# Second attention: the maximum of a head pair as two reductions of one PSUM bank, with scores and shifted scores issued head by head

## The chip, the core and the metric

The kernel runs on one core of a Trainium2 chip. The metric is device time in microseconds, the median of several executions. The engines that matter are TensorE (matmuls; PE in the rows, PEld its weight loads), VectorE (DVE), ScalarE (ACT) and GpSimd (POOL). They run side by side and meet by semaphores. PSUM, where matmuls write, has eight banks of 512 fp32 values in each of 128 partitions. TensorE's clock has two levels here, 1.2 and 2.4 GHz; the profile shows the granted one as a share of 2.4.

## What is computed

Eight sequences of 256 tokens with 128 features pass four stages, each a normalisation, a layer and a residual: an attention by hyperbolic distance, a mixture of experts, a second attention, and the mixture again. Only the second attention is touched:

```python
def _L0_attn_b_ref(x, qkv_w, qkv_b, proj_w, proj_b):
    B, N, D = x.shape
    H, hd = (NHEAD, HEAD_DIM)          # 16, 8
    qkv = x @ qkv_w.T + qkv_b
    ...
    q = q * cos + _rotate_half(q) * sin
    k = k * cos + _rotate_half(k) * sin
    attn = jnp.einsum('abhqd,abhkd->abhqk', q, k) * hd ** (-0.5)
    attn = jax.nn.softmax(attn, axis=-1)
    out = jnp.einsum('abhqk,bhkd->abhqd', attn, v)
    out = jnp.swapaxes(out, 1, 2).reshape(B, N, D)
    return out @ proj_w.T + proj_b
```

The softmax subtracts each query's maximum over its 256 keys. The kernel computes all scores twice for that: once with the queries on the partitions, to take the maximum along the free axis, and once with the keys on the partitions and the maximum already subtracted inside the matmul (`q2` holds the queries with an extra row of minus the maximum). The second form is what the exponential and the product with the values need.

## The kernel before

The order of work is written out by hand: each engine has its own program, and semaphores tie them. The second attention handles 8 samples (sequences) with 16 heads of 8 features. Heads go in pairs, `UNITS` = 8 pairs a sample, 64 in all. A head lies in a strip of 32 partitions, and a tile matmul uses 32 rows of TensorE's array: pair U uses row groups `j0` and `j0 + 1`, where `j0` is 0 for even pairs and 2 for odd ones.

TensorE (`samples_b`, line 728) first scores `AHEAD` = 13 pairs. Then in step U it issues the shifted scores of pair U and the scores of pair V = U + 13 (`b_tiles`, line 671), half of a value product for pair U - 3 or U - 4 (`pv_b`, line 719: eight matmuls), and, at three steps of every eight, a part of the maxima of a sample (`b_max_step`): a transpose, then two selections that spread the maxima over the rows of `q2`.

Scores go to banks 0 and 1, one for each head of the pair, with the two halves of the queries side by side (`b_score_step`, line 659). These banks are single: the next pair's scores wait until VectorE has read them (`s_mx`). Shifted scores go to banks 2 and 3 or 4 and 5, alternating (`b_shifted_step`, line 665), and wait for ScalarE's exponential of two pairs before (`s_e`). V and U have opposite parity, so that scores and shifted scores of one step lie on different row groups.

VectorE (`samples_b`, line 1501) reduces banks 0 and 1 in one instruction (`head_max`, line 1502) and, between the pairs, does the small work on the maxima: `max_split` after the eighth pair, `max_rows` after the next, and `shift` (an addition of 128x512 from PSUM) after the two that follow. ScalarE takes the exponential of the pair's 1024 columns (line 1009) and every fourth step copies a product out (line 1000). GpSimd and the DMA queues have no work that the stage waits for.

Of the kernel before, what the change touches and what calls it, by code (L numbers as in the profile page):

```python
# [7 lines left out]
ALU = mybir.AluOpType  # L8
ACT = mybir.ActivationFunctionType
AX_X = mybir.AxisListType.X  # L10
# [12 lines left out]
UNITS = H // 2  # L23
CHUNKS = H // 4
MT = N // P
# [36 lines left out]
def hybrid(nc, x, consts, wA, wB, bqk, brow, rwT, wexp, out):  # L62
    ctx = ExitStack()

    def sem(name):
        return ctx.enter_context(nc.semaphore(name))
# [3 lines left out]
    with ctx:  # L70
# [26 lines left out]
        def bank(n, k=1):  # L97
            return ps[:, 512 * n:512 * (n + k)]

        with ExitStack() as att:  # L100
# [40 lines left out]
            with ExitStack() as att_b:  # L141
                def sb_(name, shape, dt=F32):
                    return att_b.enter_context(nc.sbuf_tensor(name, shape, dt))
                q2 = [sb_(f"q2{k}", [P, CHUNKS, N], F32R) for k in range(2)]
                mx = sb_("mx", [P, CHUNKS, 4, MT])
# [135 lines left out]
        s_s1 = sem("b_scores_in_psum")  # L281
        s_mx = sem("b_max_read")
# [5 lines left out]
        s_s2 = sem("b_shifted_in_psum")  # L288
# [51 lines left out]
        def tok(s, m=0, n=N):  # L340

            return slice(s * N + m, s * N + m + n)
# [85 lines left out]
        def _(pe):  # L428
            def mm(o, l, r, start=True, stop=True, **kw):
                return pe.matmul(o, l, r, start=start, stop=stop, **kw)  # L430

            def rows(j):
                return slice(32 * j, 32 * (j + 1))
# [225 lines left out]
            def b_score_step(U, nt, i):  # L659

                s, c, j0 = U // UNITS, U % UNITS // 2, 2 * (U % 2)
                return mm(bank(i)[:, nt * N:(nt + 1) * N], qt[rows(j0 + i), c, tok(s, nt * P, P)],
                          kt[rows(j0 + i), c, tok(s)], tile_position=(32 * (j0 + i), 0))

            def b_shifted_step(U, mt, i):

                s, c, j0 = U // UNITS, U % UNITS // 2, 2 * (U % 2)
                return mm(bank(2 + 2 * (U % 2) + i)[:, mt * N:(mt + 1) * N], kt[rows(j0 + i), c, tok(s, mt * P, P)],
                          q2[s % 2][rows(j0 + i), c, :], tile_position=(32 * (j0 + i), 0))

            def b_tiles(U, V):

                shifted, scores = 0 <= U < B * UNITS, V < B * UNITS
                if shifted and U % UNITS == 0:
                    pe.wait_ge(s_q2, 2 * (U // UNITS) + 2)
                if shifted and U >= 2:
                    pe.wait_ge(s_e, U - 1)
                if scores and V >= 1:
                    pe.wait_ge(s_mx, V)
                for half in range(MT):  # L680
                    if shifted:
                        b_shifted_step(U, half, 0)
                        last = b_shifted_step(U, half, 1)
                        if half == MT - 1:
                            last.then_inc(s_s2, 1)
                    if scores:
                        b_score_step(V, half, 0)
                        last = b_score_step(V, half, 1)
                        if half == MT - 1:
                            last.then_inc(s_s1, 1)  # L690

            def b_max_transposed(s):

# [34 lines left out]
            def samples_b():  # L728
                for V in range(AHEAD):
                    b_tiles(-1, V)  # L730
                    b_max_step(V)
                for U in range(B * UNITS + 3):
                    V = U + AHEAD
                    b_tiles(U, V)
                    if U >= 3:
                        pv_b((U - 3) // 2, (U - 3) % 2)
                    if V < (B + 1) * UNITS:
                        b_max_step(V)
# [519 lines left out]
        def _(dve):  # L1258
# [242 lines left out]
            def samples_b():  # L1501
                def head_max(U):
                    c, j0 = U % UNITS // 2, 2 * (U % 2)
                    dve.wait_ge(s_s1, U + 1)
                    dve.tensor_reduce(mx[:, c, j0:j0 + 2, :], bank(0, 2).rearrange("p (i t m) -> p i t m", i=2, t=MT),  # L1505
                                      AX_X, ALU.max).then_inc(s_mx, 1)

                def max_split(s):

                    dve.wait_ge(s_mx, UNITS * (s + 1))  # L1510
                    if s >= 1:
                        dve.wait_ge(s_mT, s)
                    rows = mtok[:, :, :].rearrange("p t (j x) -> p t j x", x=32)[:, :, :, 0:8]
                    rows = rows.rearrange("p t j (c e) -> p t j c e", e=2)
                    whole = mx[:, :, :, :].rearrange("p c j t -> p t j c")
                    st.do(dve.tensor_scalar(rows[:, :, :, :, 0], whole, -1.0, None, ALU.mult))
                    st.sync()
                    for t in range(MT):
                        last = dve.scalar_tensor_tensor(rows[:, t, :, :, 1], whole[:, t], -1.0, rows[:, t, :, :, 0],
                                                        ALU.mult, ALU.subtract)  # L1520
                    last.then_inc(s_ms, 1)

                def max_rows(s):
                    dve.wait_ge(s_mT, s + 1)
                    if s >= 1:
                        dve.wait_ge(s_mq, 2 * s)
                    dve.tensor_copy(mxT[:, :], bank(7)[:, 0:N]).then_inc(s_mr, 1)

                def shift(s, half):
                    dve.wait_ge(s_mq, 2 * s + half + 1)  # L1530
                    if s >= 2:
                        dve.wait_ge(s_s2, UNITS * (s - 1))
                    cs = slice(2 * half, 2 * half + 2)
                    dve.tensor_tensor(q2[s % 2][:, cs, :], bank(7).rearrange("p (c n) -> p c n", c=2),  # L1534
                                      qt[:, cs, tok(s)], ALU.add).then_inc(s_q2, 1)

                dve.wait_ge(s_sel, 3)
                for V in range((B + 1) * UNITS):
                    if UNITS <= V < B * UNITS and V % UNITS == 0:
                        dve.wait_ge(s_ms, V // UNITS)  # L1540
                    if V < B * UNITS:
                        head_max(V)
                    s, at = V // UNITS - 1, V % UNITS
                    if at == UNITS - 1 and V < B * UNITS:
                        max_split(s + 1)
                    elif at == 0 and s >= 0:
                        max_rows(s)
                    elif at in (1, 2) and s >= 0:
                        shift(s, at - 1)
# [265 lines left out]
```

## Time and profile before

| | us |
|---|---|
| median of 3 runs | 1306.38 (1305.45 to 1308.87) |
| the profiled execution | 1306.9 |
| its span, first to last instruction | 1305.1 |
| TensorE busy / VectorE busy / ScalarE busy over the span | 1015.4 / 1020.3 / 735.0 |
| VectorE's maxima of the second attention (line 1505) | 64 x 1224 ns, 78.3 busy |
| VectorE idle ahead of them, most of it until TensorE is done | 40.7 |
| ScalarE's exponentials (line 1009) | 64 x 1023 ns, 65.4 busy, 58.7 idle ahead of them |

The profile is one execution. The second attention's scores begin near 779 us and its last value product ends near 944. The busy shares over the whole span say little about it, since the two mixtures of experts fill most of the time with dense matmuls; it has to be read in its own stretch. Idle time is put down to the instruction that ended it. Durations of matmuls overlap: the distance between starts tells the pace, and a matmul's own row holds its way through the array too.

### The profile page before, as it was taken

Reading aid. Unit: us, or ns where it says so; the run is one execution under the profiler, and the core shown is the slowest. Engines: PE = TensorE matmul, PEld = TensorE weight load, DVE = VectorE, ACT = ScalarE, POOL = GpSimd, SP = SyncE. Lnnn points to the kernel's source line nnn. Section 1 sums busy time; section 2 is a strip of 40 time slices with the busy share of each in tenths; the row PEclk is TensorE's granted clock in tenths of the full one; section 3 lists DMA queues with packets and bytes.
Section 4 is the critical chain, followed back from the end, with each engine's and each line's share of the span. In section 5 each row is a group of like instructions: output and inputs, shape, how many; then the busy total and the mean of one; then the engine's idle time right before and its main releaser. Section 6 shows DMA issues by size and latency. Waiting matters only on the chain. (4 is left out here: it accounts for less than half of the span.)

```text
span 1305.1 us, 17528 instructions
## 1 busy us (share of the span) xinstructions
PE 1015.4 (78%) x5292; PEld 706.6 (54%) x5292; DVE 1020.3 (78%) x1720; ACT 735.0 (56%) x886; POOL 324.0 (25%) x217
## 2 busy tenths in 40 slices
PE   4655666666643799999999664778962899999997
PEld 3433333334322577787777332333451777877776
DVE  4347988888827799999998766666157799999997
ACT  2323999999952355555555221555521555555554
POOL 2002655555530122222222320000000122222221
PEclk8665555555555799999999775776575899999999
DMA  1000000000000366666664000000000566666664
GB/s 48 1 1 0 1 1 1 1 1 1 1 7 8 91 153 153 148 150 149 145 149 94 29 1 0 1 2 1 1 7 8 130 152 146 148 149 140 146 149 103
DMA packets 26090, 85.24 MB, mean 65 GB/s; under 512 B 3904, under 2 KB 17088, under 8 KB 17856
## 3 DMA queue, kind: packets, MB, share of 16 engines
q1 hardware_dynamic: 26048, 84.70, 28.4%
q8 instruction: 25, 0.41, 0.1%
q14 instruction: 17, 0.14, 0.0%
HBM read 82.58 MB, written 2.10 MB: 65 GB/s over the span
## 5 line engine op out<-in xcount | busy, mean ns | idle before, releaser
L1061 ACT ACTIVATE sg<-ps 128x512 f32<-128x512 f32 x264 | 157.8, 599 | 127.3 <-PE ps L430 127.3
L1067 ACT ACTIVATE hh<-hf 128x512 fp32r<-128x512 f32 x264 | 167.0, 633 | 104.6 <-DVE hf L1691 104.3
L430 PE MATMUL ps<-xh,whi 128*128 128x512 f32 x528 | 207.6, 393 | 0.0
L430 PE MATMUL ps<-xh,wlo 128*128 128x512 f32 x528 | 207.4, 393 | 0.0
L430 PE MATMUL ps<-xl,whi 128*128 128x512 f32 x528 | 207.0, 392 | 0.0
L1685 DVE TENSOR_TENSOR hl<-hf,hh 128x512 fp32r<-128x512 f32 x264 | 186.3, 706 | 26.3 <-ACT hh L1067 6.7
L1165 POOL TENSOR_TENSOR rr<-xr,rr 128x2048 f32<-128x2048 f32 x32 | 144.9, 4545 | 211.9 <-ACT xr L952 207.7
L1691 DVE TENSOR_TENSOR hf<-h,cbc 128x512 f32<-128x512 f32 x256 | 195.0, 762 | 0.0
L1678 DVE TENSOR_TENSOR h<-sg,ps 128x512 f32<-128x512 f32 x264 | 179.4, 680 | 18.3 <-PE ps L430 8.1
L1209 POOL CAST whi<-wraw 128x384 fp32r<-128x384 f32 x66 | 61.7, 935 | 480.3 <-PE ps L430 377.6
L430 PE MATMUL ps<-hh,whi 128*128 128x512 f32 x264 | 110.7, 419 | 7.8 <-DVE hl L1685 7.8
L430 PEld LDWEIGHTS ps<-xh,whi 128*128 128x128 f32 x528 | 100.0, 189 | 23.0 <-DVE h L1678 0.5
L430 PEld LDWEIGHTS ps<-xl,whi 128*128 128x128 f32 x528 | 100.0, 189 | 22.2
L430 PEld LDWEIGHTS ps<-xh,wlo 128*128 128x128 f32 x528 | 99.7, 189 | 21.7
L1505 DVE TENSOR_REDUCE mx<-ps 128x4 f32<-128x1024 f32 x64 | 78.3, 1224 | 40.7 <-PE ps L430 39.9
L430 PE MATMUL ps<-hl,whi 128*128 128x512 f32 x264 | 103.8, 393 | 0.0
L430 PE MATMUL ps<-hh,wlo 128*128 128x512 f32 x264 | 103.8, 393 | 0.0
L1009 ACT ACTIVATE wr<-ps 128x1024 f32<-128x1024 f32 x64 | 65.4, 1023 | 58.7 <-PE ps L430 58.3
L1211 POOL TENSOR_TENSOR wlo<-wraw,whi 128x384 fp32r<-128x384 f32 x66 | 87.7, 1329 | 5.3
L430 PE MATMUL ps<-qt,kt 32*128 32x256 f32 x256 | 50.8, 494 | 45.6 <-DVE xr L1368 44.9
L1368 DVE TENSOR_SCALAR xr<-ps 128x1024 f32<-128x1024 f32 x64 | 77.8, 1215 | 8.6 <-PE ps L430 8.6
L1376 DVE SCALAR_TENSOR_TENSOR xr<-ps,xr 128x1024 f32<-128x1024 f32 x64 | 78.2, 1221 | 4.3
(246 smaller groups left out, 1590.5 us busy)
## 6 DMA issues: line engine op xcount, KB each, us to landing
cbc<-routing_coefficients SPq DMA_DIRECT2D x128, 512.0 KB, 6.1
wraw<-in_wexp_dram SPq DMA_DIRECT2D x66, 192.0 KB, 5.9
X<-in_x_dram SPq DMA_DIRECT2D x4, 256.0 KB, 4.5
routing_coefficients<-cT SPq DMA_DIRECT2D x8, 128.0 KB, 2.3
out_dram<-X SPq DMA_DIRECT2D x4, 256.0 KB, 2.8
cstb<-in_consts_dram SPq DMA_DIRECT2D x1, 648.0 KB, 3.5
wa<-in_wA_dram SPq DMA_DIRECT2D x1, 256.0 KB, 3.9
wb<-in_wB_dram SPq DMA_DIRECT2D x1, 192.0 KB, 3.6
```

The lines of the kernel that those rows point to most:

```text
L430: return pe.matmul(o, l, r, start=start, stop=stop, **kw)
L1009: act.activation(wr[:, C % CHUNKS, U % 2 * UC:(U % 2 + 1) * UC], bank(2 + 2 * (U % 2), 2), ACT.Exp, scale=SCALE_B).then_inc(s_e, 1)
L1061: act.activation(sg[c % 2][:, :], bank(4 + 2 * (c % 2)), ACT.Silu).then_inc(s_sg, 1)
L1067: act.activation(hh[c][:, :], hf[c % 2][:, :], ACT.Copy).then_inc(s_hh, 1)
L1165: pool.tensor_tensor(rr[:, C % RR, :], xr[:, C % XR, :], rr[:, C % RR, :], ALU.add).then_inc(s_S, 1)
L1211: pool.tensor_tensor(wlo[slot][:, :], wraw[slot][:, :], whi[slot][:, :], ALU.subtract).then_inc(s_ws, 1)
L1368: dve.tensor_scalar(xr[:, C % XR, at], bank(0, 2), 0.0, None, ALU.max).then_inc(s_N, 1)
L1376: dve.scalar_tensor_tensor(xr[:, C % XR, at], bank(2, 2), R_MAX, xr[:, C % XR, at], ALU.min, ALU.mult).then_inc(s_X, 1)
L1505: dve.tensor_reduce(mx[:, c, j0:j0 + 2, :], bank(0, 2).rearrange("p (i t m) -> p i t m", i=2, t=MT), AX_X, ALU.max).then_inc(s_mx, 1)
L1678: dve.tensor_tensor(h1[c % 2][:, :], sg[c % 2][:, :], bank(5 + 2 * (c % 2)), ALU.mult).then_inc(s_h1, 1)
L1685: dve.tensor_tensor(hl[c][:, :], hf[c % 2][:, :], hh[c][:, :], ALU.subtract).then_inc(s_hl, 1)
L1691: dve.tensor_tensor(hf[c % 2][:, :], h1[c % 2][:, :], coefs, ALU.mult).then_inc(s_h, 1)
```

## The change

`head_max` takes the maximum by two reductions of one bank each, and raises `s_mx` after each, so that it counts heads. `s_s1` is raised after each head's scores. TensorE issues score and shifted score of head 0 for both halves, then, after another wait for `s_mx`, those of head 1. In the old order both heads' tiles of a half stood together, behind one wait. The counts of the waits follow: `max_split` waits for twice as many. No buffer, no other loop and no DMA changes.

```diff
@@ -675,19 +675,18 @@
                     pe.wait_ge(s_q2, 2 * (U // UNITS) + 2)
                 if shifted and U >= 2:
                     pe.wait_ge(s_e, U - 1)
-                if scores and V >= 1:
-                    pe.wait_ge(s_mx, V)
-                for half in range(MT):
-                    if shifted:
-                        b_shifted_step(U, half, 0)
-                        last = b_shifted_step(U, half, 1)
-                        if half == MT - 1:
-                            last.then_inc(s_s2, 1)
-                    if scores:
-                        b_score_step(V, half, 0)
-                        last = b_score_step(V, half, 1)
-                        if half == MT - 1:
-                            last.then_inc(s_s1, 1)
+                for i in range(2):
+                    if scores and V >= 1:
+                        pe.wait_ge(s_mx, 2 * (V - 1) + i + 1)
+                    for half in range(MT):
+                        if scores:
+                            last = b_score_step(V, half, i)
+                            if half == MT - 1:
+                                last.then_inc(s_s1, 1)
+                        if shifted:
+                            last = b_shifted_step(U, half, i)
+                            if half == MT - 1 and i == 1:
+                                last.then_inc(s_s2, 1)
 
             def b_max_transposed(s):
 
@@ -1501,13 +1500,14 @@
             def samples_b():
                 def head_max(U):
                     c, j0 = U % UNITS // 2, 2 * (U % 2)
-                    dve.wait_ge(s_s1, U + 1)
-                    dve.tensor_reduce(mx[:, c, j0:j0 + 2, :], bank(0, 2).rearrange("p (i t m) -> p i t m", i=2, t=MT),
-                                      AX_X, ALU.max).then_inc(s_mx, 1)
+                    for i in range(2):
+                        dve.wait_ge(s_s1, 2 * U + i + 1)
+                        dve.tensor_reduce(mx[:, c, j0 + i, :], bank(i).rearrange("p (t m) -> p t m", t=MT),
+                                          AX_X, ALU.max).then_inc(s_mx, 1)
 
                 def max_split(s):
 
-                    dve.wait_ge(s_mx, UNITS * (s + 1))
+                    dve.wait_ge(s_mx, 2 * UNITS * (s + 1))
                     if s >= 1:
                         dve.wait_ge(s_mT, s)
```

## Rows read from the trace of the kernel before

**Rows 1.** Chain of work that ended last, 778 to 950 us, shares by line.

```profile
by line: PE ps L430 51.5%; DVE mx L1505 35.8%; issue 4.4%; PE ps L698 2.5%; PE ps L748 2.3%; DVE q L1534 1.8%; ACT o_all L1000 0.4%; DVE b_otok L1561 0.3%; DVE b_rden L1557 0.2%; DVEq L1504 0.0%; DVEq L1554 0.0%
```

**Rows 2.** Timeline, pairs ahead: start, duration, engine, line, operation, count, idle and its releaser.

```profile
783.69 0.80 PE L430 MATMUL ps<-kt,qt 32*128 32x256 f32 x4 [1.32 <-DVE mx L1505]
784.53 1.23 DVE L1505 TENSOR_REDUCE mx<-ps 128x4 f32<-128x1024 f32 x1 [0.89 <-PE ps L430]
785.81 0.80 PE L430 MATMUL ps<-kt,qt 32*128 32x256 f32 x4 [1.32 <-DVE mx L1505]
```

**Rows 3.** First tiles of the first and of the 52nd step (chain, timeline).

```profile
807.12 0.85 PE ps L430 x8
...
916.74 0.79 PE L430 MATMUL ps<-q,kt 32*128 32x256 f32 x4
```

**Rows 4.** Timeline, a plain step at a granted clock of 0.50.

```profile
826.29 0.58 PE L430 MATMUL ps<-q,kt 32*128 32x256 f32 x2 [0.43 <-DVE mx L1505]
...
827.02 1.08 PE L430 MATMUL ps<-wr,vt 128*32 128x256 f32 x8
827.12 1.02 ACT L1009 ACTIVATE wr<-ps 128x1024 f32<-128x1024 f32 x1 [1.22 <-PE ps L430]
827.17 1.23 DVE L1505 TENSOR_REDUCE mx<-ps 128x4 f32<-128x1024 f32 x1 [1.02 <-PE ps L430]
...
828.54 0.58 PE L430 MATMUL ps<-q,kt 32*128 32x256 f32 x2 [0.43 <-DVE mx L1505]
```

**Rows 5.** Timeline of TensorE at a granted clock of 1.00, a selection and plain steps.

```profile
818.39 0.39 PE L430 MATMUL ps<-q,kt 32*128 32x256 f32 x2
...
818.83 0.64 PE L430 MATMUL ps<-wr,vt 128*32 128x256 f32 x8
819.40 0.50 PE L430 MATMUL ps<-mxT,mxs 128*128 128x256 f32 x2
820.34 0.39 PE L430 MATMUL ps<-q,kt 32*128 32x256 f32 x2 [0.44 <-DVE mx L1505]
...
822.30 0.39 PE L430 MATMUL ps<-q,kt 32*128 32x256 f32 x2 [0.88 <-DVE mx L1505]
```

**Rows 6.** Timeline of TensorE at 0.50: selections of two neighbouring steps.

```profile
902.82 0.80 PE L430 MATMUL ps<-mxT,mxs 128*128 128x256 f32 x2
...
905.28 0.80 PE L430 MATMUL ps<-mxT,mxs 128*128 128x256 f32 x2
```

**Rows 7.** Timeline of TensorE in the tail: products of two steps, and the closing run.

```profile
928.52 1.08 PE L430 MATMUL ps<-wr,vt 128*32 128x256 f32 x8
...
930.25 1.08 PE L430 MATMUL ps<-wr,vt 128*32 128x256 f32 x8
...
940.97 3.40 PE L430 MATMUL ps<-wr,vt 128*32 128x256 f32 x32
```

**Rows 8.** Timeline of VectorE: an addition of 128x512, the reduction behind it, a small operation.

```profile
818.35 0.69 DVE L1534 TENSOR_TENSOR q<-ps,qt 128x512 fp32r<-128x512 f32 x1
...
818.97 1.23 DVE L1505 TENSOR_REDUCE mx<-ps 128x4 f32<-128x1024 f32 x1
...
830.67 0.19 DVE L1516 TENSOR_SCALAR mtok<-mx 128x32 fp32r<-128x32 f32 x1
```

**Rows 9.** Timeline of TensorE in the preparation: two steps, each for four row groups.

```profile
755.92 0.51 PE L430 MATMUL ps<-b_qh,sel 32*128 32x512 f32 x4
756.26 0.41 PE L430 MATMUL ps<-b_ql,sel 32*128 32x512 f32 x4
```

**Rows 10.** Busy us by stretch: PE, PEld, DVE, ACT, POOL, then granted clock, DMA, GB/s.

```profile
813.70:817.70 4.00, 3.93 (x34) 1.73 (x34) 2.75 (x6) 1.75 (x2) 0.00 (x0) 0.50 0.00 0
817.70:824.50 6.80, 4.54 (x64) 2.35 (x60) 5.43 (x6) 3.86 (x5) 0.00 (x0) 1.00 0.01 2
...
899.60:903.00 3.40, 3.40 (x27) 1.22 (x24) 2.69 (x3) 1.99 (x2) 0.00 (x0) 0.50 0.01 2
...
952.00:960.00 8.00, 7.23 (x56) 6.38 (x56) 4.35 (x10) 0.60 (x2) 0.00 (x0) 1.00 0.00 0
```

## Prediction

> **What bounds the kernel now.** First I read the chain that ended last, over the stretch of the second attention (778 to 950 us). TensorE's one matmul line holds 51.5% of it and the maximum on VectorE 35.8% [rows 1]: the stage is a ping-pong of these two, and ScalarE's exponentials are almost nowhere on the chain. The timeline shows three parts.
>
> Thirteen head pairs are scored ahead, until 807.1 us. A pair is four matmuls, which take 0.83 us until the reduction starts; the reduction takes 1.23, and 0.05 later TensorE begins the next four [rows 2]. Nothing overlaps: 2.12 us a pair.
>
> Then 51 steps (807.1 to 916.7 us, 109.6 us or 2.15 a step [rows 3]), each with scores of pair V, shifted scores of pair U = V - 13 and eight value products. With TensorE granted 1.2 GHz, a plain step is 2.25 us: tiles from 826.29, products from 827.02 (0.73 for eight tile matmuls), reduction at 827.17, next tiles at 828.54, which is 0.14 after the reduction's end [rows 4]. At 2.4 GHz it is 1.96 (tiles at 820.34 and 822.30): products come after 0.44 and take 0.57 to the selection behind them [rows 5], and the reduction starts 0.58 after the tiles [rows 5, 8]. Three steps in eight also carry a transpose or a selection of the maxima. At 1.2 GHz those take 2.46, and TensorE is then busy throughout [rows 6].
>
> Last, 916.7 to about 944.4 us, the steps have no scores. TensorE sets their pace at 1.2 GHz: 1.73 us each, then a run of 3.4 us of products [rows 7].
>
> **The change part by part.** *The reduction.* One instruction of 1024 elements becomes two of 512. The nearest row of that size from PSUM is the addition of 128x512, 0.69 us, and the reduction behind it started 0.62 after it did [rows 8]. Half of 1.23, 0.61, is the lower bound, 0.69 the upper. I take 0.69 for the end that TensorE sees and 0.62 for the pitch of two in a row; the same element count makes the addition a close stand-in. VectorE then needs at least 1.24 us for a pair.
>
> *Scores ahead.* Head 0 of the next pair can be computed while head 1 is reduced. A head's own loop is 0.05 + 0.83 + 0.69 = 1.57 us, above VectorE's 1.24, so a pair takes about 1.6 where it took 2.12. That holds for ten of the thirteen. The others also carry VectorE's work on the maxima, two additions of 0.69 among it, which used to lie in VectorE's idle time; I count nothing for them. 10 x 0.5 = **-5 us**.
>
> *The order of the tiles.* The old order puts tiles of four row groups side by side. The new one issues score and shifted tile of head 0, the second half of both on the same two row groups, then head 1. If TensorE kept program order, the second halves would hold up head 1, and a step would have three rounds in place of two. One row speaks on this. In the preparation the program issues columns 0 and 1 of the query highs, then 0 and 1 of the lows, and only then columns 2 and 3. The trace has all four highs at 755.92 and all four lows at 756.26 [rows 9]: work for free row groups went past work for busy ones, past a wait already met as well. So eight tiles stay two rounds, 0.73 or 0.44 us, if head 1's wait is met; if not, head 1's rounds start when it is.
> The Trainium skill says otherwise (TensorE: Matmul & The Clock Gate, Part 3, "The mechanism"): only weight loads are pulled ahead, and matmuls start and end strictly in program order. By that rule the third round would be paid, which is the third rival below; the row disagrees with it.
>
> *Plain step at 1.2 GHz.* TensorE's own work is 0.73 + 1.02 = 1.75 us (the tail's pace, 1.73 [rows 7]). Let a step start with both heads' waits met: scores are there after 0.84, head 0 is reduced by 1.53, head 1 by 2.15 to 2.2. The next step starts at 1.75, its head 1 only at about 2.2, so it ends 1.75 later, near 3.95, a length of 2.2; the one after that meets no wait. Lengths alternate 1.75 and 2.2, mean 1.97, against 2.25.
> *Steps with transpose or selection at 1.2 GHz:* TensorE is full, 2.46 stays. Eight steps: 5 x 1.97 + 3 x 2.46 = 17.2 us, against 5 x 2.25 + 3 x 2.46 = 18.6 before and 8 x 2.15 = 17.2 as the trace has it with its share of fast clock. The lower clock alone gains nothing here.
>
> *Plain step at 2.4 GHz.* Scores after 0.54 to 0.58, TensorE's own work 0.44 + 0.57 = 1.01, VectorE 1.24. The same recurrence gives lengths of 1.36 and 1.52, mean 1.44, against 1.96. The three special steps add VectorE's two additions (1.24) and some small operations (0.19 the first [rows 8]), some 1.3 of which finds no slack (an estimate: the plain steps leave VectorE 0.2 each): eight steps 8 x 1.44 + 1.3 = 12.8 us.
>
> *The clock.* It rose to 2.4 GHz at 817.7, and at a like place in four more samples, right after TensorE had been busy 3.93 of 4.00 us at the transpose; a stretch just as full (3.40 of 3.40) brought no rise [rows 10]. It fell again after 6.8 us in which TensorE was busy 4.54, that is in plain steps of 1.96 [rows 5, 10]. The change keeps the full stretches and packs the same matmuls into steps of 1.44: 4.54/6.80 x 1.96/1.44 = 0.91. The stretch from 952 to 960 held 2.4 GHz with 7.23 of 8.00, 0.90 [rows 10]. So I expect a rise at the first to third sample and then mostly no fall.
> Main part, with 4 of its 6.4 samples at 2.4 GHz: 4 x 12.8 + 2.4 x 17.2 = 92.5, against 109.6: **-17 us**.
>
> *The tail.* The new order changes nothing by itself (two row groups, two rounds). At 2.4 GHz TensorE needs 1.01 a step, and ScalarE, with 1.02 for each exponential [rows 4] and every fourth step a copy of 128x512 (no dearer than the 0.69 of rows 8), about 1.2: 13 x 0.5 + about 1.7 of the closing products = **-8 us**. If the clock is low, nothing.
>
> *The added wait.* A third wait stands inside each step, with shifted tiles, products and selections queued behind it on TensorE. One wait costs 0.05 after its release [rows 2], two 0.14 [rows 4]. Met early it costs nothing; at 0.05 on each of some 60 steps **+3 us**, bound 0 to 0.14 each, 9 us. ScalarE's exponential waits for head 1's tiles: at most 0.5 late, and its 1.02 leaves over 0.9 idle in each plain step before [rows 4].
>
> Sum: -5 - 17 - 8 + 3 = -27 us. The profiled execution took 1306.9 us, 1305.1 of it the span; the median of the runs shown is 1306.4, so the forecast is 1306.4 - 27 = **1279 us**.
>
> **The rivals.** *1. The clock falls again in every sample.* For it: the old kernel did just that, 6.8 us high of the 17.2 of eight steps, two fifths. Eight steps take 1/(0.4/12.8 + 0.6/17.2) = 15.1 us, the main part 96.7: -13, -5 ahead, 0 in the tail, +3: **1292 us**. Against it: the denser steps.
> *2. It never rises.* -5 + 0 + 0 to 3: **1303 us**. For it: the stretch at 899.6, full and without a rise; against it five rises in seven samples.
> *3. Program order holds on TensorE.* A third round costs half of the two rounds' 0.73, 0.36 us at 1.2 GHz. A plain step is 1.75 + 0.36 = 2.11, a special one 2.82: eight steps 19.0, main part 6.4 x 19.0 = 121 (+12), tail 13 x 0.36 = +5, ahead -5, and I leave the clock low: **1318 us**. It decides against the change as soon as a second pair of row groups can't start beside the first. For it: the skill's rule; against it rows 9.
>
> **How the numbers follow.** Forecast 60%, rival 1 17%, rival 2 10%, rival 3 10%, the rest 3% for a wait inside the step that costs the whole gain. The low end is the high clock from the first sample with a free wait: 6.4 x 12.8 = 82 in the main part, 1306.4 - 28 - 5 - 8 = 1265. The high end takes in rivals 1 and 2: 1304. A measurement tells 0.3% (4 us) from no change: rivals 1 and the forecast are faster, rival 2 lies on the border, rival 3 is slower. Faster 81%, same 8%, slower 11%.
>
> **What would show it.** Right: reductions of 0.6 to 0.69 at twice the count; about 1.6 a pair ahead; eight tiles still 0.73 or 0.44 before the products; steps alternating; granted clock high through most of the stage and its tail; all else unmoved. Wrong: tiles in three rounds (1.1 at 1.2 GHz), reductions well over 0.69, or a clock that still falls in each sample.

## The result, and the profile after

The changed kernel takes 1267.1 us in the median of four executions (1263.9 to 1286.9), the kernel before beside it 1305.9: a ratio of 0.970, 95% interval 0.966 to 0.973. The forecast of 1279 had the sign and lies 12 us too high; the range of 1265 to 1304 holds the result. This ratio and those below leave out executions more than 1.5% above the fastest of the same kernel, here the one of 1286.9; the medians keep them.

I compare the two profiled executions (1306.9 and 1268.4 us; spans 1305.1 and 1266.5) by the points at which TensorE starts a new part, as in [rows 2, 3, 7]:

| part, us | before | after | forecast | measured |
|---|---|---|---|---|
| all before the first scores | 779.4 | 777.2 | 0 | -2.2 |
| 13 pairs ahead | 27.8 | 21.6 | -5 | -6.2 |
| 51 steps | 109.6 | 89.6 | -17 | -20.0 |
| tail | 28.3 | 19.5 | -8 | -8.8 |
| the added wait | | | +3 | inside the 51 steps |
| all behind | 360.0 | 358.6 | 0 | -1.4 |
| span | 1305.1 | 1266.5 | -27 | -38.6 |

So 35 of the 38.6 us come from the stage. The start of the first scores lies between 775 and 784 us in all the profiles here, changed or not, so the -2.2 in front of it is no effect of the change.

The page of the changed kernel gives the reductions and, by slices of 31.7 us, the granted clock. The stage fills the slices 25 to 29:

```profile
PEclk8665555555555599999999986589965999999999
L1505 DVE TENSOR_REDUCE mx<-ps 128x2 f32<-128x512 f32 x128 | 82.4, 686 | 11.6 <-PE ps L430 10.6
```

128 reductions of 0.686 us stand where 64 of 1.23 stood [rows 2]. The chain that ended last, over 778 to 911 us:

```profile
by line: PE ps L430 56.6%; DVE mx L1505 19.0%; issue 8.1%; DVE q L1534 4.1%; ACT wr L1008 2.6%; ACT o_all L999 2.3%; PE ps L747 1.7%; PE ps L697 1.7%; DVE mxT L1527 1.1%; ACT L1008 1.0%; DVE mtok L1519 0.7%; DVE mtok L1516 0.6%; DVE b_otok
```

The reduction held 35.8% of that chain [rows 1] and holds 19.0% now. The ping-pong shows as gone in the timeline of the pairs ahead (start, duration, engine, line, operation, count, idle and its releaser):

```profile
783.56 1.39 PE L430 MATMUL ps<-kt,qt 32*128 32x256 f32 x4 [0.18 <-DVE mx L1505]
784.38 1.29 DVE L1505 TENSOR_REDUCE mx<-ps 128x2 f32<-128x512 f32 x2 [0.28 <-PE ps L430]
785.13 1.39 PE L430 MATMUL ps<-kt,qt 32*128 32x256 f32 x4 [0.18 <-DVE mx L1505]
```

A pair is 1.57 us (783.56 to 785.13) where it was 2.12. TensorE idles 0.18 a pair instead of 1.32, VectorE 0.28 instead of 0.89 [rows 2]. Both reductions together take 1.29, hardly more than the old one's 1.23.

Next, TensorE in two plain steps at a granted clock of 0.50 (1.2 GHz), with the reductions between:

```profile
815.94 0.58 PE L430 MATMUL ps<-kt,qt 32*128 32x256 f32 x1
...
815.96 0.57 PE L430 MATMUL ps<-q,kt 32*128 32x256 f32 x1
...
816.32 0.41 PE L430 MATMUL ps<-kt,qt 32*128 32x256 f32 x1
...
816.68 1.08 PE L430 MATMUL ps<-wr,vt 128*32 128x256 f32 x8
816.77 1.29 DVE L1505 TENSOR_REDUCE mx<-ps 128x2 f32<-128x512 f32 x2 [0.87 <-PE ps L430]
...
817.69 0.58 PE L430 MATMUL ps<-kt,qt 32*128 32x256 f32 x1
...
818.07 0.41 PE L430 MATMUL ps<-kt,qt 32*128 32x256 f32 x1
...
818.12 0.58 PE L430 MATMUL ps<-kt,qt 32*128 32x256 f32 x1
...
818.84 1.08 PE L430 MATMUL ps<-wr,vt 128*32 128x256 f32 x8
...
819.85 0.58 PE L430 MATMUL ps<-kt,qt 32*128 32x256 f32 x1
```

The first step starts with both heads' waits met: first halves at 815.94 to 815.96, second halves at 816.32, products at 816.68, 0.74 after the first tile. Its length is 1.75. The second starts head 0 at 817.69, but head 1 only at 818.12, just after VectorE has left that bank, and lasts 2.16. These are the alternating 1.75 and 2.2 of the prediction; the old step was 2.25 [rows 4].

The same at 1.00 (2.4 GHz):

```profile
858.35 0.38 PE L430 MATMUL ps<-kt,qt 32*128 32x256 f32 x1
...
858.70 0.38 PE L430 MATMUL ps<-kt,qt 32*128 32x256 f32 x1
...
858.89 2.63 DVE L1505 TENSOR_REDUCE mx<-ps 128x2 f32<-128x512 f32 x4 [0.25 <-PE ps L430]
...
859.73 0.35 PE L430 MATMUL ps<-kt,qt 32*128 32x256 f32 x1
...
860.23 0.38 PE L430 MATMUL ps<-kt,qt 32*128 32x256 f32 x1
...
861.23 0.38 PE L430 MATMUL ps<-kt,qt 32*128 32x256 f32 x1
```

The steps start at 858.35, 859.73 and 861.23: 1.38 and 1.50, forecast 1.36 and 1.52, before 1.96 [rows 5]. VectorE runs four reductions in 2.63 and then idles 0.25 (from 861.52 to 861.77) until TensorE has the next tiles: it is busy for nine tenths of two steps and sets most of their pace, where TensorE and VectorE took turns before.

The clock, as busy time by stretch (columns as in [rows 10]):

```profile
777.00:799.00 22.00, 18.99 (x60) 13.66 (x62) 18.52 (x33) 0.00 (x0) 4.50 (x1) 0.50 0.00 0
799.00:831.30 32.30, 30.35 (x232) 15.40 (x232) 23.95 (x43) 17.62 (x19) 0.00 (x0) 0.50 0.00 1
831.30:888.00 56.70, 54.95 (x596) 29.81 (x598) 53.21 (x96) 40.24 (x45) 0.00 (x0) 1.00 0.01 2
888.00:907.80 19.80, 16.30 (x194) 7.67 (x186) 3.11 (x8) 16.31 (x19) 0.00 (x0) 1.00 0.00 1
```

It rose once, at 831.0, as the 16th of the 51 steps began (in the third sample whose scores fall into them), and stayed at 2.4 GHz through the steps and the tail. Before, it rose in five samples and fell in each.

### The profile page after: what moved, and what is told of

It is laid out like the page before. It is cut to its first block and busy times, and to the rows that moved or that the text cites. A ratio compares the mean times of both kernels' runs of the same rounds, so it can differ in the third digit from the quotient of the medians.

```text
span 1266.5 us, 17592 instructions
## 1 busy us (share of the span) xinstructions
PE 1006.7 (79%) x5292; PEld 714.6 (56%) x5292; DVE 1023.3 (81%) x1784; ACT 734.1 (58%) x886; POOL 324.2 (26%) x217
## 5 line engine op out<-in xcount | busy, mean ns | idle before, releaser
L1505 DVE TENSOR_REDUCE mx<-ps 128x2 f32<-128x512 f32 x128 | 82.4, 686 | 11.6 <-PE ps L430 10.6
L1008 ACT ACTIVATE wr<-ps 128x1024 f32<-128x1024 f32 x64 | 65.3, 1024 | 32.2 <-PE ps L430 32.0
```

The costliest lines, as they stand in the source:

```text
L1008: act.activation(wr[:, C % CHUNKS, U % 2 * UC:(U % 2 + 1) * UC], bank(2 + 2 * (U % 2), 2), ACT.Exp, scale=SCALE_B).then_inc(s_e, 1)
L1505: dve.tensor_reduce(mx[:, c, j0 + i, :], bank(i).rearrange("p (t m) -> p t m", t=MT), AX_X, ALU.max).then_inc(s_mx, 1)
```

## The experiments

Two theories stood at first. Mine: the reductions and the order of the tiles together let the engines overlap, and the denser TensorE keeps the clock, which then pays most. The rivals: the order alone costs (a third round of tiles), or the split alone gains, or the clock is the whole gain. Where a kernel carries extra matmuls, their results go to banks that are rewritten before anybody reads them.

**The order alone, with the old reduction** (against the kernel before).

```diff
                 if scores and V >= 1:
                     pe.wait_ge(s_mx, V)
-                for half in range(MT):
-                    ...
+                for i in range(2):
+                    for half in range(MT):
+                        if scores:
+                            last = b_score_step(V, half, i)
+                            ...
+                        if shifted:
+                            last = b_shifted_step(U, half, i)
```

> The kernel before with the new order of the tiles alone: one reduction of 1024 elements, one wait for it ahead of the step, then score and shifted tile of head 0 for both halves, then head 1. Theory (free row groups pass busy ones): eight tiles stay two rounds, 0.73 us at 1.2 GHz before the products, a plain step stays 2.25 or 1.96, time within 0.3% of before. Rival (program order holds): a third round of 0.36 us in each of 64 steps at 1.2 GHz, some 20 us slower.

Measured: 1307.5 us (median of 10, 1301.5 to 1312.2) beside 1307.5 for the kernel before, ratio 0.999 (0.996 to 1.001). TensorE at the start of one step, at 0.50:

```profile
833.70 0.58 PE L430 MATMUL ps<-kt,qt 32*128 32x256 f32 x1
833.71 0.58 PE L430 MATMUL ps<-q,kt 32*128 32x256 f32 x1
833.72 0.58 PE L430 MATMUL ps<-kt,qt 32*128 32x256 f32 x1
833.72 0.57 PE L430 MATMUL ps<-q,kt 32*128 32x256 f32 x1
834.08 0.41 PE L430 MATMUL ps<-kt,qt 32*128 32x256 f32 x1
...
834.10 0.41 PE L430 MATMUL ps<-kt,qt 32*128 32x256 f32 x1
```

The program issues head 0's first halves, head 0's second halves, then head 1's. The four first halves of both heads start within 0.02 us, the second halves 0.38 later. The rows don't name the head, but one pair of row groups runs one round at a time: in the changed kernel, where head 1 had to wait, head 0's second halves at 818.07 follow its first ones at 817.69 by 0.38. So four tiles at once are both heads', and head 1's first halves went past head 0's second ones, whose row groups were taken. Two rounds stay two, and the third rival (1318) is out. So is, for row-tiled matmuls, the sentence of the Trainium skill that the prediction set against it (TensorE: Matmul & The Clock Gate, Part 3, "The mechanism"): in strict program order head 1's tiles would have waited.

**The split alone, with the old order and one wait for both heads** (against the changed kernel).

```diff
-                for i in range(2):
-                    if scores and V >= 1:
-                        pe.wait_ge(s_mx, 2 * (V - 1) + i + 1)
-                    ...
+                if scores and V >= 1:
+                    pe.wait_ge(s_mx, 2 * V)
+                for half in range(MT):
+                    ...
```

> Two reductions of one bank with the old order of the tiles, and TensorE waits for both ahead of the step. Theory (the gain is the overlap of a head's scores with the other head's reduction): no gain, VectorE needs 1.29 us for a pair in place of 1.23, so 0.06 x 64 = 4 us slower. Rival (smaller reductions alone free the banks sooner): faster.

Measured: 1316.4 us (10; 1310.1 to 1323.1), ratio 1.007 (1.004 to 1.010): 9 us slower, where 4 were expected. A plain step at 0.50:

```profile
851.99 0.58 PE L430 MATMUL ps<-q,kt 32*128 32x256 f32 x2 [0.49 <-DVE mx L1506]
...
852.85 1.29 DVE L1506 TENSOR_REDUCE mx<-ps 128x2 f32<-128x512 f32 x2 [1.01 <-PE ps L430]
...
854.28 0.58 PE L430 MATMUL ps<-q,kt 32*128 32x256 f32 x2 [0.49 <-DVE mx L1506]
```

2.29 a step against 2.25: the 0.06 by which two reductions outlast one, some 4 us in 64 pairs. In this profile, the slowest of the ten executions, the clock also never rose in the stage, which took 176.0 us against 165.7; so the missing bursts of high clock can account for the rest, which one profile doesn't prove. Neither the order nor the split gains anything alone. With the wait per bank added to both, TensorE refills bank 0 while bank 1 is read. The wait was not taken apart from the order: a wait per bank in the old order, where head 0's second half is issued behind head 1's first, was not run.

**Extra full-width matmuls among the pairs ahead,** to have the clock up before the steps begin; on the changed kernel (shown) and, twice after each pair, on the one before.

```diff
+                    if U < 0:
+                        fill(2 * V + i)
+            def fill(n):
+                mm(bank(2 + n % 4), kt[:, 0, 0:P], qt[:, 0, 0:2 * N])
```

> The changed kernel with two matmuls of 128x128 by 512 columns added to each pair that is scored ahead, into banks that nobody reads and that the shifted scores overwrite later. They serve no result. Theory (the clock is the larger part of the gain, and the denser steps keep it): it rises to 2.4 GHz during the 13 pairs ahead and stays, the pairs take about 1.35 us, all 51 steps about 1.6 on average; 1255 to 1259 us, some 10 below the changed kernel. Rival (the clock depends on chance or falls again for another reason): within 3 us of the changed kernel, or slower by what the added matmuls take, 13 x 2 x 0.2 to 0.4 us.

> The kernel before with the same added matmuls in the pairs ahead. Theory (plain steps of 1.96 us do not keep the clock): it is high in the pairs ahead, 3 to 4 us gained there, and falls in the steps as before; 1301 to 1305 us. Rival (a clock once high stays high whatever the steps are): main part 51 x 2.0 = 102 and tail 19, 1285 us or less.

Measured: 1286.6 (4; 1282.5 to 1292.1) and 1305.9 (10; 1303.9 to 1311.1), beside 1307.5. The aim was missed. TensorE of the first of them:

```profile
790.57 0.79 PE L430 MATMUL ps<-kt,qt 32*128 32x256 f32 x2
791.29 0.80 PE L430 MATMUL ps<-qt,kt 128*128 128x512 f32 x1
```

Row tiles and full-width matmuls follow each other at 0.72, a pair takes 2.9 us instead of 1.57, and the clock stayed at 0.50 until 829 us although TensorE was busy 39.00 of the 39.00 us from 781 to 820. The part ahead grew to 38.9 us; but with the clock up from 829 on, the 51 steps took 83.6 and the tail 19.5. On the kernel before, four of the five bursts of high clock came as they had (from 834.3, 851.4, 868.4 and 885.5 us), the first, at 817.7, did not, and the stage took 168.0. That run tells nothing on a clock that is once high, since it never was in the part ahead.

**The changed kernel again,** in two further sets of executions, to see how steady it is.

> The changed kernel, unchanged, for more executions beside the next three. Theory (the gain hangs on when the granted clock rises, which differs between executions): its times spread more than the 0.3% of before, from about 1264 to 1290 us, median near 1267. Rival (one disturbed execution among four): all within 0.3% of 1267.

> The changed kernel once more beside the two, on the same chip: 1263 to 1287, median near 1270.

Measured: 1273.6 (6; 1263.4 to 1286.3), ratio 0.974 (0.970 to 0.978), and 1278.3 (4; 1268.1 to 1294.7), ratio 0.973 (0.968 to 0.979). The first set was a favourable draw. Over all 14 executions it lies between 1263.4 and 1294.7, median 1269.6, where all executions of the kernel before lie between 1301 and 1319, with medians of 1306 to 1309. The granted clock over the whole span mostly goes with it: 0.797 at 1268.1, 0.774 at 1286.5, 0.760 at 1294.7, though 0.786 at 1286.9. The slowest is a profile in which the clock never rose in the stage; its steps and its tail by stretch:

```profile
797.50:907.00 109.50, 107.53 (x830) 52.23 (x832) 79.58 (x139) 59.28 (x64) 0.00 (x0) 0.50 0.00 1
907.00:935.00 28.00, 27.42 (x186) 11.78 (x186) 2.47 (x7) 15.87 (x19) 0.00 (x0) 0.50 0.00 1
```

Here the 51 steps take 109.3 us, the tail 28.6, the part ahead 21.6: the gain in the steps and the tail is gone and the -6 ahead is left. This is the second rival, which the prediction gave one chance in ten, at 1303 us; of the 12 us by which this execution is faster than the profiled one before, 6 lie outside the stage. With the clock low throughout, the steps of the split alone took 119.1, and eight steps of the order alone at 0.50 took 18.46 (824.65 to 843.11) where eight take 17.3 here, 7 us over 51 steps. So the overlap is worth 7 to 10 us in the steps even at 1.2 GHz; the kernel before had its 109.6 with a mean granted clock of 0.66.

**The kernel before with its clock kept up** by extra value products that change nothing: 8 to 16 after each pair ahead and 8 in each plain step.

```diff
+            def fill(n, where):
+                for k in range(n):
+                    j = k % 4
+                    mm(bank(where)[rows(j), ...], vt[:, 0, 0:VW],
+                       kt[:, 0, 0:N].bitcast(F32), tile_position=(0, 32 * j))
...
                     b_tiles(-1, V)
+                    fill(16 if V < 3 else 8, 6)
...
+                    if V < B * UNITS and V % UNITS >= 3:
+                        pe.wait_ge(s_q2, 2 * (V // UNITS))
+                        fill(8, 7)
```

> The kernel before, with the same added matmuls in the pairs ahead and 8 more in each of the five plain steps of a sample, into the bank of the maxima while that is free. They serve no result. Theory (clock and overlap are two gains, and the clock alone is worth less): granted clock high throughout, plain steps 1.96, main part 101 us in place of 110, tail 19 in place of 28; 1285 to 1290 us, so 20 to 25 slower than the changed kernel. Rival (the clock is all of the gain): 1270 or less. If the clock does not stay high, a plain step costs 2.8 and the kernel is some 20 us slower than before.

Measured: 1285.0 us (4; 1283.6 to 1288.4) beside 1306.3, ratio 0.984 (0.982 to 0.986). Its steps, and a step at a granted clock of 1.00:

```profile
803.00:903.00 100.00, 89.48 (x1356) 46.09 (x1356) 74.47 (x89) 59.07 (x64) 0.00 (x0) 1.00 0.01 2
```

```profile
852.13 0.39 PE L430 MATMUL ps<-q,kt 32*128 32x256 f32 x2
...
852.71 1.22 DVE L1515 TENSOR_REDUCE mx<-ps 128x4 f32<-128x1024 f32 x1 [0.73 <-PE ps L430]
...
853.03 1.04 PE L430 MATMUL ps<-kt,vt 128*32 128x256 f32 x16
854.08 0.39 PE L430 MATMUL ps<-q,kt 32*128 32x256 f32 x2
```

The old step stays at 1.95, as in [rows 5], and the 16 products lie in TensorE's idle time. The clock alone is worth 21 us: 99.8 in the steps, 18.6 in the tail. The changed kernel in the same set took 1273.6, 11 us less, with plain steps of 1.44 and pairs of 1.57 for 1.95 and 2.12. That the clock is the whole gain is refuted.

Four profiles of these experiments, set side by side, part the two gains. The stage, from its first scores to the part behind it, took, in us:

| | clock never high | clock high in the steps and the tail |
|---|---|---|
| no overlap | 176.0 (split alone) | 146.3 (before, kept up) |
| overlap | 159.5 (changed, slowest) | 127.2 (changed, clock up from the second step, last experiment) |

The overlap is worth 16.5 us at the low clock (some 4 of them the split's own price) and 19.1 at the high one, the clock 29.7 and 32.3. Both gains stand by themselves, and the clock is the larger. The kernel before (165.7) already had part of it from its bursts.

**The same extra products in the part ahead of the changed kernel only.**

```diff
                     b_tiles(-1, V)
+                    fill(16 if V < 3 else 8, 6)
```

> The changed kernel with added matmuls in the shape of the value products (8 of them 1.02 us at 1.2 GHz, 0.57 at 2.4) in the pairs scored ahead, 16 for each of the first three pairs and 8 for each later one, into the bank of the products, which nobody reads yet. They serve no result. In fill_ahead the added 128x512 matmuls took 0.73 us apiece, the pairs ahead 2.9 us in place of 1.6, and the clock stayed at 1.2 GHz there. Theory (the clock is most of the gain, the dense steps keep it): the first three pairs 2.8 us each, then the clock rises, pairs 1.35, all 51 steps 1.6 on average from the first one; main part 83 us in place of 90, stage some 5 us shorter than the changed kernel, 1260 to 1265, with little spread. Rival (no rise ahead): the pairs take 1.75 to 2.8, 4 to 6 us slower than the changed kernel.

Measured: 1275.4 us (5; 1270.3 to 1278.0), ratio 0.976 (0.974 to 0.978), worse than hoped. By stretch:

```profile
782.00:809.00 27.00, 24.71 (x310) 13.25 (x302) 21.73 (x40) 4.40 (x5) 0.00 (x0) 1.00 0.01 2
809.00:847.00 38.00, 38.00 (x299) 18.09 (x296) 27.90 (x50) 20.31 (x22) 0.00 (x0) 0.51 0.00 1
847.00:900.00 53.00, 50.75 (x546) 27.21 (x546) 47.17 (x86) 37.61 (x41) 0.00 (x0) 1.00 0.01 2
```

The clock was high through the pairs ahead (which cost 26.8 us instead of 21.6, with the extra work), fell at 809.0, just behind the first three steps, which have no products yet (TensorE was busy 2.22 of 4.50 us from 803.2), and came back at 846.5 only, though TensorE was busy 38.00 of 38.00 us between. Here a high clock was lost where the program thins out, and full work alone didn't bring it back soon.

**All shifted tiles ahead of the waits** in the changed kernel, to see whether their place between the heads matters.

```diff
+                for i in range(2):
+                    for half in range(MT):
+                        if shifted:
+                            last = b_shifted_step(U, i, half)
+                            ...
                 for i in range(2):
                     if scores and V >= 1:
                         pe.wait_ge(s_mx, 2 * (V - 1) + i + 1)
                     for half in range(MT):
                         if scores:
                             ...
-                        if shifted:
-                            ...
```

> The changed kernel with all four shifted tiles ahead of the scores and of their waits. Theory (free row groups pass busy ones, so the place of the shifted tiles does not matter): pace of the steps unchanged, 1.37 and 1.51 at 2.4 GHz, time within 4 us of the changed kernel. Rival (the shifted tiles between the heads are what fills the wait): plain steps 0.2 to 0.4 us longer, 10 to 20 us slower.

Measured: 1282.2 us (4; 1275.9 to 1290.0), ratio 0.981 (0.978 to 0.986), against 1273.6 for the changed kernel beside it. Two stretches of its steps:

```profile
848.00:855.00 7.00, 6.89 (x74) 3.73 (x70) 6.93 (x12) 4.65 (x6) 0.00 (x0) 1.00 0.00 1
853.00:860.00 7.00, 6.90 (x62) 3.20 (x64) 5.29 (x9) 4.29 (x5) 0.00 (x0) 0.65 0.01 2
```

At 2.4 GHz its eight steps take 13.0 us, as many as the changed kernel's 12.9; but its clock rose at 824.3, fell at 855, after TensorE had been busy 6.89 of 7.00 us, and stayed down. So a TensorE as busy as the changed kernel's (54.95 of 56.70) doesn't always keep the clock. Its steps took 100.1 and its tail 28.1. The place of the shifted tiles costs nothing directly; the loss of this profile is all clock. Whether the order causes the fall, or the four executions drew badly, four executions can't say, with 14 of the changed kernel spread over 31 us.

**Keeping the clock up in the changed kernel.** First with extra products from the part ahead on (8, or 16 after the first two pairs), 8 in each of the three steps without products and 4 in every plain step with scores; then the same without those in the part ahead.

```diff
                     b_tiles(-1, V)
+                    fill(16 if V < 2 else 8, 6)
...
+                    if U < 3:
+                        fill(8, 6)
+                    if V < B * UNITS and V % UNITS >= 3:
+                        if V % UNITS == 3:
+                            pe.wait_ge(s_q2, 2 * (V // UNITS))
+                        fill(4, 7)
```

> The changed kernel with added matmuls in the shape of the value products, which serve no result: 16 for each of the first two pairs ahead and 8 for each later one, 8 in each of the first three steps (which have no products of their own), and 4 in each plain step (0.28 us at 2.4 GHz, inside TensorE's idle time of a step of 1.44). fill_pv lost the high clock at its first three steps and got it back 38 us later. Theory (the clock is what varies between executions, and steps that keep TensorE fed hold it): high clock from the pairs ahead to the end of the tail in each execution, pairs ahead 24 us, 51 steps 83 us, 1260 to 1264, and a spread under 5 us where the changed kernel spreads by 23. Rival (the added work costs more than the clock gives): 1270 or more, with little spread.

> The same without the added matmuls in the pairs ahead, which then stay at 1.2 GHz and 21.6 us. Theory: the clock rises within the first steps, which cost 2.2 to 2.5 each until then, and stays; 51 steps 86 us, 1262 to 1267, little spread. Rival (the rise needs the stretch at a transpose): like the changed kernel, a rise as late as 830 us or later, 1265 to 1285.

Measured: 1273.2 (6; 1271.1 to 1279.8), ratio 0.973 (0.971 to 0.976), and 1274.0 (5; 1272.4 to 1277.6), ratio 0.972 (0.970 to 0.975), beside 1278.3 for the changed kernel in the same set. Of the first, 1260 to 1264 was expected; the rival of 1270 or more came true. The clock holds from 783.6 in the one and from 809.5 in the other, through the tail, and the spread shrinks from 27 us to 9 and 5. In the first three steps, where the extra products in the part ahead alone had lost it, TensorE is now busy 5.60 of 5.60 us from 805. But the gain is eaten elsewhere. TensorE of the first:

```profile
858.76 0.38 PE L430 MATMUL ps<-kt,qt 32*128 32x256 f32 x1
...
860.01 0.62 PE L430 MATMUL ps<-kt,vt 128*32 128x256 f32 x8
860.55 0.38 PE L430 MATMUL ps<-kt,qt 32*128 32x256 f32 x1
```

This step is 1.79 (858.76 to 860.55), the next 1.52, where the changed kernel has 1.51 and 1.37. Behind head 1's tiles, which wait for VectorE, eight products and the four extra ones take 1.00 (859.55 to 860.55 in the same view), so they push the next step's tiles back: they no longer lie in idle time as they did in the old step of 1.96.

**Extra products only until the clock is up:** none in the part ahead, 8 in each of the first three steps, 4 in the plain ones of the first eight.

```diff
+                    if U < 3:
+                        fill(8, 6)
+                    if U < UNITS and V % UNITS >= 3:
+                        if V % UNITS == 3:
+                            pe.wait_ge(s_q2, 2 * (V // UNITS))
+                        fill(4, 7)
```

> The changed kernel with added matmuls, which serve no result, in its first eight steps alone: 8 in each of the first three, 4 in each plain one. In kept_from_first_step they brought the rise at 810 us, but 4 in each plain step of the whole main part made plain steps 1.79 and 1.52 in place of 1.51 and 1.37. Theory (only the rise is left to chance, once high the changed kernel's own steps hold the clock): pairs ahead 21.6, first eight steps 17.5, the other 43 at 1.61 on average, 69: main part 87, tail 19.5; 1262 to 1267 median and a spread under 8 us. Rival (its own steps lose the clock in some executions too): some executions at 1275 or more, a median like the changed kernel's.

Measured: 1263.8 us (5; 1261.5 to 1267.4) beside 1306.5, ratio 0.967 (0.965 to 0.970). By stretch:

```profile
780.00:801.00 21.00, 17.39 (x59) 12.22 (x54) 17.23 (x29) 1.11 (x1) 4.50 (x1) 0.50 0.00 0
801.00:808.00 7.00, 6.33 (x46) 3.70 (x45) 4.03 (x7) 2.31 (x2) 0.00 (x0) 0.50 0.01 2
808.00:890.00 82.00, 79.68 (x888) 42.77 (x884) 75.33 (x136) 56.22 (x61) 0.00 (x0) 0.99 0.01 2
```

The clock rises at 810.0, in the second step, and the bare steps of 1.37 and 1.51 then hold it. The 51 steps take 86.2 us, the tail 19.5. It beats the changed kernel's median of 1269.6 by 6 us; against the best executions of that kernel (1263.4) it gains nothing; what it does is to come near them in all five executions, with a spread of 6 us for 31. The two were not run side by side. Eight of the 14 executions of the changed kernel were below 1271 too, so five in a row would come by chance once in some 16 times; that no execution of the three variants with a high clock from the first steps on, 16 in all, went above 1280, where four of the 14 did, is the stronger sign.

## Why the prediction was right, and where its sizes were off

- *The reduction*, 0.62 to 0.69 with a pitch of 0.62: 0.682 singly, 1.29 for two, a pitch of 0.61. Half of the old one was the right bound for the pitch, the addition of [rows 8] for the end of one.
- *The pairs ahead*, 1.6: 1.57. The head's own loop sets it, as worked out. -6.2 against -5, since a pair saved 0.55 where the sum took 0.5, and the three pairs that carry the work on the maxima gained too.
- *Two rounds of tiles*: held, with both waits met (815.94 and 816.32) and with the order alone. That one step of the preparation [rows 9] carried the case against the third rival, and it was enough.
- *Step lengths*: 1.75 and 2.16 against 1.75 and 2.2; 1.38 and 1.50 against 1.36 and 1.52; eight steps 12.9 against 12.8 at 2.4 GHz, 17.3 against 17.2 at 1.2. The sum at 1.2 GHz hides an error that the plain steps make up for: the step in which VectorE prepares the maxima takes 2.8 there (and 2.13 at 2.4 GHz), where I had kept 2.46. VectorE's three small operations delay the reductions; the transpose of the same step stands behind products that wait for ScalarE's copy as well, and how much each of the two costs I didn't separate. The start of that step on VectorE (start, duration, engine, line, operation, count):

```profile
850.20 0.19 DVE L1516 TENSOR_SCALAR mtok<-mx 128x32 fp32r<-128x32 f32 x1
...
850.42 0.27 DVE L1519 SCALAR_TENSOR_TENSOR mtok<-mx,mtok 128x16 fp32r<-128x16 f32 x2
...
850.73 1.29 DVE L1505 TENSOR_REDUCE mx<-ps 128x2 f32<-128x512 f32 x2
```

- *The clock*, up at the first to third sample and then held: it rose at 831.0, in the third sample, and fell no more. High for 36 of the 51 steps, or 4.5 samples, where the sum took 4: with the forecast's own eight steps that is 4.5 x 12.8 + 1.9 x 17.2 = 90 against 92.5. But this was the likeliest case and not the only one; among 14 executions three lie at 1286 and one at 1294.7, so the time hangs on something the program doesn't fix. And the reason given for the holding, that steps with TensorE busy for nine tenths keep the clock as the stretch from 952 to 960 did, is not borne out as a rule: with the shifted tiles first it fell after 6.89 of 7.00. That the clock held in the profiled execution was in part luck; what decides it stays open.
- *The tail*: -8.8 against -8. Every fourth step waits for a copy on ScalarE, as in the sum; one of them on TensorE, whose other steps here are 1.00 to 1.01:

```profile
900.39 0.64 PE L430 MATMUL ps<-wr,vt 128*32 128x256 f32 x8 [0.70 <-ACT o_all L999]
```

- *The added wait*, +3: this is the term that failed. The step lengths above come out as the recurrence gave them without it, so it costs nothing that can be seen. The recurrence already held the wait that isn't met early (it let head 1's tiles start only once VectorE had left the bank, at about 2.2), and the met ones are free: a step with all its waits met takes 1.75, the old tail's steps, which have no wait for VectorE, 1.73 [rows 7]. I charged that wait twice.

In sum, the stage was forecast at -27 and gave -35.0. Of the 8 us between, 3 are the added wait, 1.2 the pairs ahead and 0.8 the tail. The other 3 lie in the steps (-20.0 against -17), nearly all by the longer high clock, as above. The remaining 3.6 us of the 38.6 lie outside the stage and aren't the change's. How near a measured median comes to the forecast depends on the draw as well: the three sets of the changed kernel gave 1267.1, 1273.6 and 1278.3 against the 1279.

## What to carry to other kernels

When two engines hand a buffer back and forth, split the consumer's read together with the wait and the order of issue: here the order alone brought nothing (0.999), the split alone a loss (1.007), and split, order and a wait per bank together 0.970. Before costing such a change, ask which clock the denser engine will be granted: here the overlap at the low clock was worth 7 to 10 us in the steps, about as much as the kernel before already had there from its bursts of high clock, and most of the gain in the steps and the tail came with the clock staying up. If the clock holds once it is up, help it up with spare work in the first few steps, not in all the steps that have become tight (1263.8 against 1273 and 1274).

## What the runs showed of the hardware that I had not expected

- A TensorE that is busy all the time can stay at 1.2 GHz: 38.00 of 38.00 us at 0.51, 107.53 of 109.50 at 0.50, 39.00 of 39.00 at 0.50, all of it small tile matmuls with full-width ones among them; while steps with 54.95 of 56.70 busy, at 2.4 GHz already, kept it. What decides the rise isn't settled here, nor what decides the fall: 6.89 of 7.00 busy went before one, 2.22 of 4.50 before another.
- One and the same program spreads over 31 us (1263.4 to 1294.7). Three of its executions were profiled: the clock rose at 831.0 and 830.5 us, and the stage took 130.7 and 130.6, or it never rose there, and the stage took 159.5. That the executions between (1278 to 1287) had a later rise or a fall wasn't seen in a profile.
- Matmuls on free row groups start before earlier ones on busy row groups: four within 0.02 us of each other, 0.36 to 0.38 ahead of the next four.
- Two reductions of 512 elements from PSUM in a row take 1.29 us, one of 1024 1.23, and one alone 0.68: back to back the two overlap by about 0.07 (2 x 0.68 - 1.29).
- A full-width matmul of 512 columns between row tiles takes 0.72 us at 1.2 GHz from its start to that of the next tiles (791.29 to 792.01).
